# GpSimd multiplies the second halves of eight late units, from copies that ScalarE makes of the y banks

## The chip, the cores and the metric

One core of a Trainium2 chip. The metric is the device time of one execution in microseconds; the median of the runs is compared. TensorE is the matrix engine (PE in the profile), VectorE is DVE, ScalarE is ACT, GpSimd is POOL, SyncE is SP.

## The reference, cut to what matters

A recommendation tower: 40 embedding tables are looked up for 512 samples, every pair of the 40 fields goes through its own 32x32 matrix, and the 780 results with 16 dense features go through three layers. All of it is float32.

```python
e = jnp.stack([tbl_0[ids[:, 0]], ..., tbl_39[ids[:, 39]]], axis=1)   # 512 x 40 x 32
z = jnp.einsum('bpd,pde,bpe->bp', e[:, iidx, :], bilinear_matrices, e[:, jidx, :])   # 780 pairs
h = jnp.concatenate([z, dense_ctx], axis=1)
h = jnp.maximum(h @ W_top1 + b_top1, 0.0)
h = jnp.maximum(h @ W_top2 + b_top2, 0.0)
y = h @ W_top3
```

## The kernel before, in words

The 40 fields are put in 10 groups of four (`GROUPS`, `G`); a group transposed to 128 partitions (4 fields x 32) by 512 samples is one `xt[:, t, :]`. Four groups (`HOT_POS` 0, 1, 3, 5) have small tables and are looked up by one-hot matmuls on TensorE (L515), whose 0/1 columns VectorE makes (L409; four of them ScalarE, L369 and L372). The other six (`GATHER_POS` 2, 4, 6, 7, 8, 9) are gathered by GpSimd: 96 indirect DMAs (L301), 16 to a group, in one row. VectorE then turns such a group with one transpose (L425, the step "turn").

The pairs are done in 50 units (`UNIT`), each a pair of groups (t, u). For unit k TensorE makes y = matrices x xt[u] as four results of 128x512 in float32 (L546): they are two halves, 2k and 2k+1, and a half lies in two PSUM banks. There are three places for halves (`Y_SLOTS`), so half h needs the place of half h-3 (L544). VectorE multiplies each half of 128x1024 by xt[t] into `prod` (L449, 100 instructions), and TensorE sums the products over the 32 rows of each field into z_ps with a selecting matrix (L561, the step "sum"). `prod` has room for four units.

The order is written down as a list (`schedule`): unit k, then sum k-2 (`LAG`), then what `AFTER` puts behind unit k: one-hot rounds, and in the last third the parts of the first layer ("l1", L467 called from L527) on blocks of z that are ready. Behind the sum of the last of eight units ScalarE copies z_ps to z_t (L385, the step "z"); it also takes out the first part of the first layer (L382). VectorE has its own list with the same units in order, the turns (before units 0, 8, 18, 24, 32 and 38) and the "joins" of the first layer (L430). Groups 8 and 9 are t in the last 18 units: unit 32 is (8, 0), unit 33 is (8, 1), up to (8, 7) in unit 39; 40 to 47 are (9, 0) to (9, 7); 48 and 49 are the inner pairs.

Each engine runs its instructions in order. On GpSimd nothing follows the 96 gathers. The tail after unit 49 is the rest of the three layers.

Of the kernel before, what the change touches and what calls it, by code (L numbers as in the profile page):

```python
# [11 lines left out]
ALU = mybir.AluOpType  # L12
# [37 lines left out]
UNIT = []  # L50
# [6 lines left out]
MIX_RING = 2  # L57
# [2 lines left out]
       (2, 0, 3 * DIM, False), (2, 3 * DIM, P, True)]  # L60
HEAD_AFTER = 4


Y_SLOTS = 3
PROD_UNITS = 4
# [28 lines left out]
def first_unit(t):  # L94
# [11 lines left out]
    "l1": [18, 24, 26, 27, 28, 28, 31, 32, 33, 34, 36, 37, 41, 41, 43, 44, 46, 47, 48, 49],  # L106
    "turn": [0, 8, 18, 24, 32, 38],
}


def last_unit(b):
# [55 lines left out]
def bass_dlrm_tower(nc, ids, rows, hot_ids, numbers, negatives, hot_tables, dense, mats, w1, b1, w2, b2, w3, select, out):  # L167
# [23 lines left out]
    vector_rounds = [j for j in range(len(ROUND)) if j not in BY_SCALAR]  # L191
    scalar_rounds = [j for j in range(len(ROUND)) if j in BY_SCALAR]

    def mix_slot(g, s):

        return GROUPS + 3 * (g % (2 * MIX_RING)) + s if s < G - 1 else g ^ 1

    with ExitStack() as ctx:
# [30 lines left out]
        table = sb("table", [P, HOTS, G, MAX_ROWS * DIM])  # L229
        rest = sb("rest", [P, PIECE_RING, G, MAX_ROWS * DIM])  # L230
        low = sb("low", [P, PIECE_RING, G, MAX_ROWS * DIM], BF16)

        layer_cols = hot_id[:].rearrange("p o c -> p (o c)").bitcast(F32)
        h1 = layer_cols[:, 0:M1 * BATCH].rearrange("p (m b) -> p m b", m=M1)
# [42 lines left out]
        t_out = sem("t_out")  # L277
        y_done = sem("y_done")
        prod_done = sem("prod_done")
        sum_done = sem("sum_done")  # L280
        z_out = sem("z_out")
        z_last = sem("z_last")
# [10 lines left out]
        @block.gpsimd  # L293
        def _(pool):
            pool.wait_ge(ids_in, 16)
            nc.gpsimd.tensor_tensor(row[:], ids_sb[:, 0, :], ids_sb[:, 1, :], ALU.add).then_inc(row_done, 1)
            pool.wait_ge(row_done, 1)
            for g in range(GATHERS):
                for c in range(CHUNKS):
                    n = g * CHUNKS + c  # L300
                    pool.indirect_dma_start(out=x_rows[:, g, c, :], out_offset=None, in_=rows,  # L301
                                            in_offset=bass.IndirectOffsetOnAxis(ap=row[:, n:n + 1], axis=0)
                                            ).then_inc(gathered[g], 16)

        @block.sync
        def _(sp):
            def load_mats(c):
                sp.dma_start(m_sb[:, MAT0[c]:MAT0[c + 1], :], mats[:, MAT0[c]:MAT0[c + 1], :]).then_inc(mats_in[c], 16)

            def load_hot_ids(o):  # L310
                sp.dma_start(hot_id[:, o, :], hot_ids[:, o, :]).then_inc(hot_id_in[o], 16)

            def load_tables(o):
                cols = slice(0, HOT_ROWS[o] * DIM)
                sp.dma_start(table[:, o, :, cols], hot_tables[:, o, :, cols]).then_inc(table_in[o], 16)

            sp.dma_start(ids_sb[:], ids).then_inc(ids_in, 16)
            load_hot_ids(0)
            load_tables(0)
            load_hot_ids(1)  # L320
            load_tables(1)
            load_mats(0)
            load_hot_ids(2)
            load_tables(2)
            for c in range(1, 4):
                load_mats(c)
            sp.dma_start(dense_sb[:], dense).then_inc(dense_in, 16)
            for o in range(3, HOTS):
                load_hot_ids(o)
                load_tables(o)  # L330
            for c in range(4, len(MAT_CHUNKS)):
                load_mats(c)
            sp.dma_start(b1_sb[:], b1).then_inc(head_in, 16)
            sp.dma_start(b2_sb[:], b2).then_inc(head_in, 16)
            sp.dma_start(w3_sb[:], w3).then_inc(head_in, 16)

            for g in range(GROUPS):
                if g == HEAD_AFTER:
                    sp.wait_ge(hot_used, len(ROUND))
                    sp.dma_start(w1_sb[:], w1).then_inc(w1_in, 16)  # L340
                    sp.dma_start(w2_sb[:], w2).then_inc(head_in, 16)
                if g >= 2 * MIX_RING:

                    sp.wait_ge(prod_done, 2 * UNIT.index((g - 2 * MIX_RING, g - 2 * MIX_RING)) + 2)
                x_there(sp, g)
                x_there(sp, g ^ 1)
                for part, p0, p1, own in MIX:
                    sp.dma_start(xt[p0:p1, mix_slot(g, part), :],
                                 xt[p0:p1, g if own else g ^ 1, :]).then_inc(mixed[g], 16)
            sp.wait_ge(y_out, 1)  # L350
            sp.dma_start(out.rearrange("(p bt) o -> p (bt o)", bt=BT), y[:]).then_inc(stored, 16)
            sp.wait_ge(stored, 16)

        @block.scalar
        def _(act):
            act.dma_start(number[:], numbers).then_inc(number_in, 16)
            act.dma_start(negative[:], negatives).then_inc(negative_in, 16)
            act.dma_start(sel[:], select).then_inc(sel_in, 16)
            for what, k in steps:
                if what == "hot":  # L360
                    for j in [j for j in scalar_rounds if BY_SCALAR[j] == k]:
                        o, r = ROUND[j]
                        n = scalar_rounds.index(j)
                        act.wait_ge(hot_id_in[o], 16)
                        act.wait_ge(negative_in, 16)
                        if n >= ONES_RING:
                            act.wait_ge(hot_used, scalar_rounds[n - ONES_RING] + 1)
                        columns = ones(j).rearrange("p f b -> p (f b)")
                        nc.scalar.activation(columns, hot_id[:, o, :], ACT.Abs,  # L369
                                             bias=negative[:, n:n + 1]).then_inc(ones_half, 1)  # L370
                        act.wait_ge(ones_half, n + 1)
                        nc.scalar.activation(columns, columns, ACT.Relu, bias=negative[:, len(BY_SCALAR):],  # L372
                                             scale=-1.0).then_inc(ones_done, 1)
                if what == "hot" and ends_bank(what, k):
                    act.wait_ge(hot_used, k + 1)
                    nc.scalar.activation(xt[:, HOT_POS[ROUND[k][0]], :], t_ps[:], ACT.Copy).then_inc(t_out, 1)  # L376
                if what == "l1" and ends_bank(what, k) and L1_STEP[k][0] == 0:
                    m = L1_STEP[k][1]
                    if m == 0:
                        act.wait_ge(head_in, 16 * 4)  # L380
                    act.wait_ge(part_done, m + 1)
                    nc.scalar.activation(h1[:, m, :], t_ps[:], ACT.Identity, bias=b1_sb[:, m:m + 1]).then_inc(t_out, 1)  # L382
                if what == "z" and k < BLOCKS - 1:
                    act.wait_ge(sum_done, last_unit(k) + 1)
                    nc.scalar.activation(z_t[:, k, :], z_ps[:], ACT.Copy).then_inc(z_out, 1)  # L385
            for m in range(M1):
                act.wait_ge(l1_added, m + 1)
                nc.scalar.activation(h1[:, m, :], h1[:, m, :], ACT.Relu).then_inc(l1_out, 1)
            for c in range(M2):
                act.wait_ge(l2_done, c + 1)  # L390
                nc.scalar.activation(h2[:, c, :], y_ps[:, L2_BANK[c], :], ACT.Relu,
                                     bias=b2_sb[:, c:c + 1]).then_inc(l2_out, 1)
            act.wait_ge(l3_done, 1)
            nc.scalar.activation(y[:], t_ps[:, 0:BT], ACT.Copy).then_inc(y_out, 1)  # L394

        @block.vector
        def _(dve):
            nc.vector.memset(prod[:, 0, 0, :], 0.0).then_inc(cleared, 1)  # L398
            dve.wait_ge(number_in, 16)
            for what, k in vector_schedule():  # L400
# [30 lines left out]
                if what == "unit":  # L431
# [9 lines left out]
                    else:  # L441
                        partners = [xt[:, t, :].unsqueeze(1).to_broadcast([P, 2, BATCH])] * 2
                    for half in range(2):
                        slot = (2 * k + half) % Y_SLOTS
                        dve.wait_ge(y_done, 2 * k + half + 1)
                        if half == 0 and k >= PROD_UNITS:

                            dve.wait_ge(sum_done, k - PROD_UNITS + 1)
                        nc.vector.tensor_tensor(prod[:, k % PROD_UNITS, 2 * half:2 * half + 2, :],  # L449
                                                y_ps[:, 2 * slot:2 * slot + 2, :], partners[half],  # L450
                                                ALU.mult).then_inc(prod_done, 1)
# [9 lines left out]
        def _(pe):  # L461
# [9 lines left out]
            def late_blocks(parts):  # L471
                for m in parts:

                    pe.wait_ge(prod_done, LATE_READ[m])
                    for b in range(LATE_BLOCK, BLOCKS - 1):
                        pe.wait_ge(z_out, b + 1)
                        by_columns(y_ps[:, LATE_BANK[m], :], w1_sb[:, b, m * P:(m + 1) * P], z_t[:, b, :],
# [13 lines left out]
            for what, k in steps:  # L491
# [39 lines left out]
                if what == "unit":  # L531
# [6 lines left out]
                    for s in range(G):  # L538
# [2 lines left out]
                        place = INNER_PLACE[s] if t == u else s  # L541
                        if s % 2 == 0 and half >= Y_SLOTS:

                            pe.wait_ge(prod_done, half - Y_SLOTS + 1)  # L544
                        rows = slice(s * DIM, (s + 1) * DIM)
                        last = nc.tensor.matmul(y_ps[:, 2 * slot + place % 2, :], m_sb[rows, k, :], xt[rows, u, :],  # L546
                                                start=True, stop=True)
# [2 lines left out]
                if what == "sum":  # L550
# [3 lines left out]
                        pe.wait_ge(sel_in, 16)  # L554
                    if r == 0 and b >= 1:
                        pe.wait_ge(z_out, b)
                    pe.wait_ge(prod_done, 2 * k + 2)
                    window = sel[:, SEL_COLS - G * r:SEL_COLS - G * r + DIM]
                    for s in range(G):
                        place = INNER_PLACE[s] if UNIT[k][0] == UNIT[k][1] else s  # L560
# [109 lines left out]
```

## Time and profile before

| what | value |
|---|---|
| median of 3 runs | 188.96 us (188.72 to 190.56) |
| span of the profiled execution | 304.4 us |
| busy PE, DVE, ACT, POOL in that span | 210.0, 159.1, 29.8, 95.4 us |
| mean granted TensorE clock in that span | 0.808 |

The profiled execution's time is given by its span alone, and that span is 115.4 us longer than the median of the runs without the profiler. How to read it: a row of the timeline is start, duration, engine, line, operation, output<-inputs, shape, how many were merged, and in brackets how long the engine was idle before it and what ended that. In the chain, which is followed back from the last instruction, a piece that lasts longer than others of its line holds a wait of TensorE.

### The profile page before, as it was taken

How to read it: one execution, taken by the hardware profiler on the slowest of the kernel's cores; microseconds unless marked ns; L12 is line 12 of the kernel's file. 1: busy time of each engine (PE TensorE's matmuls, PEld its weight loads, DVE VectorE, ACT ScalarE, POOL GpSimd, SP SyncE). 2: the span in 40 equal slices, each digit the busy share in tenths (PEclk: the TensorE clock that was granted, in tenths of full speed). 3: DMA queues.
4: the chain of work that ended last, by engine and by line, in shares of the span. 5: the costliest groups of instructions: out<-in, count | busy, mean ns of one | idle time of the engine just before them, and what ended most of it. 6: DMA issues, size and time to landing. Idle time of an engine off the chain costs nothing.

```text
span 304.4 us, 3703 instructions
## 1 busy us (share of the span) xinstructions
PE 210.0 (69%) x1590; PEld 62.3 (20%) x1590; DVE 159.1 (52%) x156; ACT 29.8 (10%) x30; POOL 95.4 (31%) x101
## 2 busy tenths in 40 slices
PE   8866443212221221106999999999999999999997
PEld 3212100000000000002433322322222223222223
DVE  2752000210000000004999999999969889898630
ACT  2905000000000000005000000000110100000032
POOL 4777777777777777500000000000000000000000
PEclk9995755555555555555999999999999999999999
DMA  7992010000100100003550097000510004300000
GB/s 238 395 411 68 13 14 13 13 13 13 15 13 14 14 13 13 11 0 98 163 155 3 8 309 202 2 0 2 156 54 0 2 0 121 89 0 2 2 0 0
DMA packets 12688, 20.19 MB, mean 66 GB/s; under 512 B 3840, under 2 KB 6784, under 8 KB 12544
## 3 DMA queue, kind: packets, MB, share of 16 engines
q1 hardware_dynamic: 9168, 18.33, 18.7%
q0 software_dynamic: 3072, 1.58, 3.2%
q8 instruction: 12, 0.20, 0.3%
q10 hardware_dynamic: 432, 0.05, 0.1%
q14 instruction: 4, 0.03, 0.0%
HBM read 12.08 MB, written 0.00 MB: 40 GB/s over the span
## 4 chain that ended last, share of the span: by engine, by line
PE 69%; issue 30%; DVE 0%; ACT 0%
PE y_ps L546 20%; PE z_ps L561 16%; PE t_ps L515 16%; PE t_ps L467 6%; PE y_ps L467 5%; PE z_ps L483 3%; PE y_ps L490 3%; PE t_ps L583 1%; DVE prod L398 0%; ACT y L394 0%
## 5 line engine op out<-in xcount | busy, mean ns | idle before, releaser
L449 DVE TENSOR_TENSOR prod<-y_ps,xt 128x1024 f32<-128x1024 f32 x100 | 115.8, 1217 | 8.1 <-PE y_ps L546 7.6
L301 POOL DMA_INDIRECT x_rows<-rows,row x96 | 94.8, 988 | 29.2 <-issue 29.0
L409 DVE TENSOR_SCALAR hot<-hot_id,number 128x2048 bf16<-128x2048 int16 x32 | 23.6, 758 | 120.3 <-remote 74.7
L546 PE MATMUL y_ps<-xt,m_sb 32*128 32x512 f32 x400 | 65.0, 640 | 0.0
L561 PE MATMUL z_ps<-prod,sel 128*32 128x512 f32 x400 | 53.2, 604 | 0.0
L515 PE MATMUL t_ps<-hot,table 128*32 128x512 bf16 x128 | 19.5, 441 | 30.3 <-issue 30.0
L546 PEld LDWEIGHTS y_ps<-xt,m_sb 32*128 32x128 f32 x400 | 22.5, 182 | 40.6 <-issue 29.4
L515 PE MATMUL t_ps<-hot,low 128*32 128x512 bf16 x128 | 20.8, 436 | 13.5 <-issue 13.1
L515 PE MATMUL t_ps<-hot,rest 128*32 128x512 bf16 x128 | 19.8, 437 | 11.9 <-issue 11.7
L467 PE MATMUL t_ps<-z_t,table 128*32 128x512 f32 x160 | 20.5, 593 | 0.0
L483 PE MATMUL z_ps<-hot_id,sel 128*32 128x512 bf16 x30 | 9.5, 427 | 15.5 <-issue 15.5
L376 ACT ACTIVATE xt<-t_ps 128x512 f32<-128x512 f32 x4 | 2.4, 597 | 149.5 <-remote 119.8
L561 PEld LDWEIGHTS z_ps<-prod,sel 128*32 128x32 f32 x400 | 8.0, 108 | 37.8 <-issue 24.1
L515 PEld LDWEIGHTS t_ps<-hot,table 128*32 128x32 bf16 x128 | 5.1, 102 | 43.3 <-issue 39.0
L385 ACT ACTIVATE z_t<-z_ps 128x512 f32<-128x512 f32 x6 | 3.6, 597 | 84.2 <-PE z_ps L561 84.2
L515 PE MATMUL t_ps<-z_t,low 128*32 128x512 bf16 x16 | 3.8, 496 | 9.2 <-issue 9.2
L515 PEld LDWEIGHTS t_ps<-hot,low 128*32 128x32 bf16 x128 | 5.4, 105 | 22.0 <-issue 19.8
L515 PEld LDWEIGHTS t_ps<-hot,rest 128*32 128x32 bf16 x128 | 5.1, 103 | 18.5 <-issue 17.1
L490 PE MATMUL y_ps<-prod 128*128 128x512 bf16 x24 | 7.8, 504 | 1.5 <-DVE prod L398 1.5
L515 PE MATMUL t_ps<-z_t,rest 128*32 128x512 bf16 x16 | 3.8, 495 | 7.1 <-issue 7.1
L372 ACT ACTIVATE z_t<-z_t,negative 128x2048 bf16<-128x2048 bf16 x4 | 8.0, 2002 | 0.1
L369 ACT ACTIVATE z_t<-hot_id,negative 128x2048 bf16<-128x2048 int16 x4 | 8.0, 1994 | 0.0
(30 smaller groups left out, 70.5 us busy)
## 6 DMA issues: line engine op xcount, KB each, us to landing
xt<-xt SPq DMA_DIRECT2D x20, 192.0 KB, 2.5
xt<-xt SPq DMA_DIRECT2D x20, 128.0 KB, 2.5
hot_id<-hot_ids SPq DMA_DIRECT2D x4, 512.0 KB, 4.2
table<-w SPq DMA_DIRECT2D x1, 1792.0 KB, 8.2
x_rows<-rows,row POOLq DMA_INDIRECT x96
table<-hot_tables SPq DMA_DIRECT2D x2, 640.0 KB
xt<-xt SPq DMA_DIRECT2D x20, 64.0 KB, 2.1
table<-hot_tables SPq DMA_DIRECT2D x2, 512.0 KB
```

Source lines behind the costliest of these rows:

```text
L301: pool.indirect_dma_start(out=x_rows[:, g, c, :], out_offset=None, in_=rows, in_offset=bass.IndirectOffsetOnAxis(ap=row[:, n:n + 1], axis= ...
L369: nc.scalar.activation(columns, hot_id[:, o, :], ACT.Abs, bias=negative[:, n:n + 1]).then_inc(ones_half, 1)
L372: nc.scalar.activation(columns, columns, ACT.Relu, bias=negative[:, len(BY_SCALAR):], scale=-1.0).then_inc(ones_done, 1)
L385: nc.scalar.activation(z_t[:, k, :], z_ps[:], ACT.Copy).then_inc(z_out, 1)
L409: nc.vector.tensor_scalar(ones(k).rearrange("p f b -> p (f b)"), hot_id[:, o, :], number[:, o, r:r + 1], None, ALU.is_equal).then_inc(hot_ ...
L449: nc.vector.tensor_tensor(prod[:, k % PROD_UNITS, 2 * half:2 * half + 2, :], y_ps[:, 2 * slot:2 * slot + 2, :], partners[half], ALU.mult). ...
L467: last = nc.tensor.matmul(bank[q * DIM:(q + 1) * DIM, :], weights[:, q * DIM:(q + 1) * DIM], columns, start=start, stop=stop, skip_group_c ...
L483: nc.tensor.matmul(z_ps[0:DIM, :], sel[:, 0:SEL_COLS].bitcast(BF16)[:, 0:DIM], hot_id[:, 1, 0:BATCH].bitcast(BF16), start=start, stop=star ...
L490: nc.tensor.matmul(y_ps[:, 0, :], zeros[:, BATCH:BATCH + P], zeros[:, 0:BATCH], start=True, stop=True)
L515: last = nc.tensor.matmul(t_ps[f * DIM:(f + 1) * DIM, :], pieces[piece][:, f, :], ones(k)[:, f, :], start=(r == 0 and piece == 0), stop=(r ...
L546: last = nc.tensor.matmul(y_ps[:, 2 * slot + place % 2, :], m_sb[rows, k, :], xt[rows, u, :], start=True, stop=True)
L561: last = nc.tensor.matmul(z_ps[s * DIM:(s + 1) * DIM, :], window, prod[:, k % PROD_UNITS, place, :], start=first, stop=(k == last_unit(b)) ...
```

## The change

Eight second halves, 2k+1 for k = 33, 35, ..., 47, are no longer multiplied by VectorE. ScalarE copies the two banks of such a half to SBUF (`y_copy`, which lies in the space of `rest`, with room for two copies), and GpSimd multiplies the copy by xt[t] in two instructions of 128x512 each. TensorE takes the place of such a half again when it is copied, and sums such a unit when both VectorE's and GpSimd's part are done. GpSimd's multiplications stand behind its 96 gathers. ScalarE's copy of unit k stands ahead of the z copy and the first-layer step that follow unit k.

The pieces are, in order: the constants, two helpers, the space of the copies, GpSimd behind its gathers, ScalarE, VectorE, and TensorE's wait in a unit and in a sum.

```diff
+POOL_HALF = {2 * k + 1 for k in range(33, 48, 2)}
+COPY_RING = 2
...
+    def half_read(engine, h):
+        if h in POOL_HALF:
+            engine.wait_ge(y_copied, halves_before(h + 1, True))
+        else:
+            engine.wait_ge(prod_done, halves_before(h + 1, False))
+
+    def unit_multiplied(engine, k):
+        engine.wait_ge(prod_done, halves_before(2 * k + 2, False))
+        if halves_before(2 * k + 2, True):
+            engine.wait_ge(pool_prod_done, halves_before(2 * k + 2, True))
...
+        y_copy = rest[:].rearrange("p o f c -> p (o f c)")[:, 0:COPY_RING * 2 * BATCH].rearrange(
+            "p (n h b) -> p n h b", n=COPY_RING, h=2)
...
+            for n, h in enumerate(sorted(POOL_HALF)):
+                k = h // 2
+                t, u = UNIT[k]
+                x_there(pool, t)
+                pool.wait_ge(y_copied, n + 1)
+                pool.wait_ge(sum_done, k - PROD_UNITS + 1)
+                for place in range(2):
+                    last = nc.gpsimd.tensor_tensor(prod[:, k % PROD_UNITS, 2 + place, :], y_copy[:, n % COPY_RING, place, :],
+                                                   xt[:, t, :], ALU.mult)
+                last.then_inc(pool_prod_done, 1)
...
             for what, k in steps:
+                if what == "unit" and 2 * k + 1 in POOL_HALF:
+                    n = halves_before(2 * k + 1, True)
+                    slot = (2 * k + 1) % Y_SLOTS
+                    act.wait_ge(y_done, 2 * k + 2)
+                    if n >= COPY_RING:
+                        act.wait_ge(pool_prod_done, n - COPY_RING + 1)
+                    elif n == 0:
+                        act.wait_ge(hot_used, len(ROUND))
+                    nc.scalar.activation(y_copy[:, n % COPY_RING, :, :], y_ps[:, 2 * slot:2 * slot + 2, :],
+                                         ACT.Copy).then_inc(y_copied, 1)
...
                     for half in range(2):
+                        if 2 * k + half in POOL_HALF:
+                            continue
...
-                            pe.wait_ge(prod_done, half - Y_SLOTS + 1)
+                            half_read(pe, half - Y_SLOTS)
...
-                    pe.wait_ge(prod_done, 2 * k + 2)
+                    unit_multiplied(pe, k)
```

GpSimd's queue in the kernel before, from its first instruction on data to its end:

```order
L296 TENSOR_TENSOR row<-ids_sb 128x96 [waits ids_in]
L301 DMA x_rows<-rows,row 128x32 [waits row_done]
L301 DMA x_rows<-rows,row 128x32 x95
L198 UNCONDITIONAL_BRANCH
```

And in the changed kernel, the same place and the first two of the eight pairs (`rest` is the space in which the copies lie):

```order
L322 TENSOR_TENSOR row<-ids_sb 128x96 [waits ids_in]
L327 DMA x_rows<-rows,row 128x32 [waits row_done]
L327 DMA x_rows<-rows,row 128x32 x95
L337 TENSOR_TENSOR prod<-rest,xt 128x512 [waits sum_done,y_copied,turned]
L337 TENSOR_TENSOR prod<-rest,xt 128x512
L337 TENSOR_TENSOR prod<-rest,xt 128x512 [waits sum_done,y_copied,turned]
L337 TENSOR_TENSOR prod<-rest,xt 128x512
```

The pairs stand behind all 96 gathers, not behind those alone that they need.

TensorE in the kernel before, from unit 35 to sum 34 (L546 is a unit's matmul, L561 a sum's, the last row is the first-layer step behind unit 36):

```order
L546 MATMUL y_ps<-xt,m_sb 128x512 [waits prod_done]
L546 MATMUL y_ps<-xt,m_sb 128x512
L546 MATMUL y_ps<-xt,m_sb 128x512 [waits prod_done]
L546 MATMUL y_ps<-xt,m_sb 128x512
L561 MATMUL z_ps<-prod,sel 32x512 [waits prod_done]
L561 MATMUL z_ps<-prod,sel 32x512 x3
L546 MATMUL y_ps<-xt,m_sb 128x512 [waits prod_done]
L546 MATMUL y_ps<-xt,m_sb 128x512
L546 MATMUL y_ps<-xt,m_sb 128x512 [waits prod_done]
L546 MATMUL y_ps<-xt,m_sb 128x512
L561 MATMUL z_ps<-prod,sel 32x512 [waits prod_done]
L561 MATMUL z_ps<-prod,sel 32x512 x3
```

The same rows in the changed kernel (L594 is the unit's matmul, L609 the sum's):

```order
L594 MATMUL y_ps<-xt,m_sb 128x512 [waits y_copied]
L594 MATMUL y_ps<-xt,m_sb 128x512
L594 MATMUL y_ps<-xt,m_sb 128x512 [waits prod_done]
L594 MATMUL y_ps<-xt,m_sb 128x512
L609 MATMUL z_ps<-prod,sel 32x512 [waits pool_prod_done,prod_done]
L609 MATMUL z_ps<-prod,sel 32x512 x3
L594 MATMUL y_ps<-xt,m_sb 128x512 [waits prod_done]
L594 MATMUL y_ps<-xt,m_sb 128x512
L594 MATMUL y_ps<-xt,m_sb 128x512 [waits prod_done]
L594 MATMUL y_ps<-xt,m_sb 128x512
L609 MATMUL z_ps<-prod,sel 32x512 [waits pool_prod_done,prod_done]
L609 MATMUL z_ps<-prod,sel 32x512 x3
```

Nothing on TensorE moves. The first half of unit 35 waits for ScalarE's copy, and the sum behind unit 35, sum 33, is the first that waits for GpSimd.

ScalarE in the kernel before, from the first-layer step behind unit 28 to its copy of z behind sum 47:

```order
L382 ACTIVATE hot_id<-t_ps,b1_sb 128x512 [waits part_done]
L385 ACTIVATE z_t<-z_ps 128x512 [waits sum_done]
L382 ACTIVATE hot_id<-t_ps,b1_sb 128x512 [waits part_done] x2
L385 ACTIVATE z_t<-z_ps 128x512 [waits sum_done] x2
```

And in the changed kernel:

```order
L428 ACTIVATE hot_id<-t_ps,b1_sb 128x512 [waits part_done]
L404 ACTIVATE rest<-y_ps 128x1024 [waits hot_used,y_done]
L431 ACTIVATE z_t<-z_ps 128x512 [waits sum_done]
L428 ACTIVATE hot_id<-t_ps,b1_sb 128x512 [waits part_done]
L404 ACTIVATE rest<-y_ps 128x1024 [waits y_done]
L404 ACTIVATE rest<-y_ps 128x1024 [waits pool_prod_done,y_done]
L428 ACTIVATE hot_id<-t_ps,b1_sb 128x512 [waits part_done]
L404 ACTIVATE rest<-y_ps 128x1024 [waits pool_prod_done,y_done] x2
L431 ACTIVATE z_t<-z_ps 128x512 [waits sum_done]
L404 ACTIVATE rest<-y_ps 128x1024 [waits pool_prod_done,y_done] x3
L431 ACTIVATE z_t<-z_ps 128x512 [waits sum_done]
```

Eight copies come in; from the third on they wait for GpSimd, and what follows them on ScalarE waits with them.

## Rows read from the trace of the kernel before

**Rows 1.** The page: span, busy time, busy tenths and clock in 40 slices.

```profile
span 304.4 us, 3703 instructions
PE 210.0 (69%) x1590; PEld 62.3 (20%) x1590; DVE 159.1 (52%) x156; ACT 29.8 (10%) x30; POOL 95.4 (31%) x101
...
POOL 4777777777777777500000000000000000000000
PEclk9995755555555555555999999999999999999999
```

**Rows 2.** Stretches: us, busy PE, PEld, DVE, ACT, POOL, clock, DMA share, GB/s.

```profile
3.50:25.00 21.50, 15.29 (x123) 5.13 (x121) 12.46 (x15) 9.57 (x6) 16.88 (x16) 0.97 1.00 374
...
5.47:150.44 144.97, 54.11 (x357) 15.67 (x355) 28.13 (x33) 18.76 (x12) 93.22 (x95) 0.60 0.24 72
28.30:139.24 110.94, 27.29 (x79) 5.27 (x71) 6.80 (x8) 0.84 (x2) 75.27 (x79) 0.52 0.08 12
```

**Rows 3.** The chain from unit 33 to unit 46: start, us, what.

```profile
237.42 1.07 PE y_ps L546 x8
...
244.34 0.99 PE z_ps L561 x8
245.34 1.45 PE y_ps L546 x8
...
247.78 0.86 PE t_ps L467 x8
...
253.63 1.45 PE y_ps L546 x8
...
256.07 1.27 PE y_ps L546 x8
...
258.33 1.30 PE y_ps L546 x8
259.64 1.00 PE z_ps L561 x8
...
264.48 1.45 PE y_ps L546 x8
...
272.77 1.45 PE y_ps L546 x8
```

**Rows 4.** Timeline of POOL, the gathers 1, 11 and 96.

```profile
3.55 1.09 POOL L301 DMA_INDIRECT x_rows<-rows,row  x1 [0.28 <-POOL row L296]
...
17.78 1.53 POOL L301 DMA_INDIRECT x_rows<-rows,row  x1 [0.30 <-issue]
...
125.99 1.37 POOL L301 DMA_INDIRECT x_rows<-rows,row  x1 [0.30 <-issue]
```

**Rows 5.** Timeline of DVE: a table split, twenty products in a row, the last turn.

```profile
17.27 1.22 DVE L418 TENSOR_TENSOR rest<-table 128x1024 f32<-128x1024 f32 x1
...
175.57 22.90 DVE L449 TENSOR_TENSOR prod<-y_ps,xt 128x1024 f32<-128x1024 f32 x20
...
252.01 0.70 DVE L425 STREAM_TRANSPOSE xt<-x_rows 128x512 f32<-128x512 f32 x1
```

**Rows 6.** Groups: line, engine, shapes, count, busy, mean ns, idle before.

```profile
L449 DVE TENSOR_TENSOR prod<-y_ps,xt 128x1024 f32<-128x1024 f32 x100 | 115.8, 1217 | 8.1 <-PE y_ps L546 7.6
...
L409 DVE TENSOR_SCALAR hot<-hot_id,number 128x2048 bf16<-128x2048 int16 x32 | 23.6, 758 | 120.3 <-remote 74.7 <-issue 32.8 <-PE t_ps L515 8.5
...
L369 ACT ACTIVATE z_t<-hot_id,negative 128x2048 bf16<-128x2048 int16 x4 | 8.0, 1994 | 0.0
...
L376 ACT ACTIVATE xt<-t_ps 128x512 f32<-128x512 f32 x4 | 2.4, 597 | 149.5 <-remote 119.8 <-PE t_ps L515 29.7
L454 DVE TENSOR_TENSOR z_t<-z_ps,dense_sb 128x512 f32<-128x512 f32 x1 | 0.7, 691 | 2.3 <-PE z_ps L561 2.3
...
L296 POOL TENSOR_TENSOR row<-ids_sb 128x96 int32<-128x96 int32 x1 | 0.4, 382 | 2.4 <-DMA ids_sb<-ids 2.4
```

**Rows 7.** Timeline of ACT: the copy of z behind sum 39.

```profile
260.70 0.60 ACT L385 ACTIVATE z_t<-z_ps 128x512 f32<-128x512 f32 x1 [8.38 <-PE z_ps L561]
```

More of the change, by code:

```diff
@@ L108, with halves_before @@
 }
+def halves_before(n, by_pool):
+    return len([h for h in range(n) if (h in POOL_HALF) == by_pool])
 def last_unit(b):
@@ L279, in bass_dlrm_tower @@
         prod_done = sem("prod_done")
+        y_copied = sem("y_copied")
+        pool_prod_done = sem("pool_prod_done")
         sum_done = sem("sum_done")
@@ L342, in _ @@
                 if g >= 2 * MIX_RING:
-                    sp.wait_ge(prod_done, 2 * UNIT.index((g - 2 * MIX_RING, g - 2 * MIX_RING)) + 2)
+                    unit_multiplied(sp, UNIT.index((g - 2 * MIX_RING, g - 2 * MIX_RING)))
                 x_there(sp, g)
@@ L472, in late_blocks @@
                 for m in parts:
-                    pe.wait_ge(prod_done, LATE_READ[m])
+                    half_read(pe, LATE_READ[m] - 1)
                     for b in range(LATE_BLOCK, BLOCKS - 1):
```

## The prediction

> **What bounds the kernel now.** I read the page first. It shows a span of 304.4 us, in which GpSimd works through the first 17 of 40 slices and TensorE runs at half its clock in most of that time [rows 1]. The runs without the profiler take 188.96 us. So the profiled execution holds some 115 us that the timed runs don't, and the next view must say where. The busy time by stretches does: from 28.3 to 139.2 us TensorE has 79 matmuls, VectorE 8 operations and ScalarE 2, while GpSimd gathers on at its even pace [rows 2]. The reader is to see that the one-hot stage is stretched in the profile and GpSimd's gathers are not. Everything about who is early or late at the units therefore has to be moved to the timed run's clock before it is used.
>
> The shift has two bounds. It is at least 304.4 - 188.96 = 115.4 us. And from VectorE's first operation on data (5.47) to the first product (150.44) VectorE is busy 28.1 of 145.0 us [rows 2]; that work can't be shorter than itself, so at most 145.0 - 28.1 = 116.8 us go. I take 116.1. That the bounds lie so close also says that the timed run has next to no other waits.
>
> The third view is the chain that ended last. From unit 33 on it is TensorE's in every piece: 1.07 us for a unit, 1.00 for a sum, 0.86 for a first-layer step. Six units last longer: 1.45, 1.45, 1.27, 1.30, 1.45 and 1.45 [rows 3], together 8.37 - 6 x 1.07 = 1.95 us. They stand where no first-layer step comes between, and VectorE, at 22.90/20 = 1.145 us a half [rows 5], needs 2.29 us for a unit against TensorE's 2.07. Elsewhere a unit with a step takes TensorE 2.93 us, and VectorE waits for it. So the late stage is bound by TensorE, and VectorE's share in it is 1.95 us.
>
> **The change, part by part.**
>
> Removed: eight multiplications of 1.217 us on VectorE [rows 6]. Only what TensorE waited for can be won. Two units without a step cost TensorE 2 x 2.07 = 4.14 us and VectorE now 3 x 1.145 = 3.4, so all six waits should go: -1.95 us. This is the most that the change can bring, 1.0%. It loses all of it if the waits had another cause.
>
> Added on ScalarE: eight copies of 128x1024 out of PSUM. The trace has 597 ns for 512 columns and 1994 for 2048 [rows 6]; on the line between them 1024 columns take 1.06 us, and the bounds are 0.60 and 1.99. That is no longer than VectorE's 1.217, and ScalarE takes the half at once, where VectorE has a backlog, so the place comes free no later. Behind the copy of unit 41 stands the copy of z that follows sum 39. The half is there when the unit's piece ends, at 258.33 + 1.30 = 259.63; the copy would end at 260.75, and z would start at 260.8 where it starts at 260.70 [rows 7]. The next reader of that z is the second of two first-layer steps, 0.86 us behind 260.64 [rows 3]. z is then there at about 261.4, the step begins at 261.5: hidden, with 0.1 us to spare. The other z copies follow theirs by several microseconds.
>
> Added on GpSimd: sixteen multiplications of 128x512 in float32. None is in the trace. The nearest row is its own two-input add of 96 columns in 382 ns [rows 6]. Taken in full proportion that is 2.04 us for 512 columns, the upper bound; VectorE's 691 ns for 512 columns [rows 6] is the lower. VectorE's two sizes, 691 for 512 and 1217 for 1024, leave 0.17 us that is fixed; with as much fixed on GpSimd, (382 - 165)/96 = 2.26 ns a column gives 0.17 + 1.16 = 1.3 us. I take that, 2.6 us for a pair. Between y and the sum a pair then costs 1.06 + 2.6 us and about 0.3 for three hand-overs (z starts 0.06 behind its sum, rows 3 and 7; I take 0.1 each): 3.96 us. In place of it TensorE has, behind unit 39, where it is tightest, sum, unit, sum and unit of 1.00 + 1.07 + 1.00 + 1.07 = 4.14 us; elsewhere one first-layer step more (5.0) or two (5.9). Hidden, once GpSimd is on time.
>
> Moved: nothing, but the pairs are queued behind all 96 gathers, and this is the term that decides. In the quiet stretch a gather is 75.27/79 = 0.95 us [rows 2] and 0.30 before the next [rows 4]; the last ends at 125.99 + 1.37 = 127.4. In the timed run GpSimd starts its gathers at the same time and has no reason to be earlier. TensorE however comes to sum 33, the first that needs a GpSimd pair, at 244.34 - 116.1 = 128.2 [rows 3]. The copy of unit 33 is long there (unit 33 ends at 238.49 - 116.1 = 122.4). So GpSimd begins its first pair when its last gather is issued and TensorE waits for both multiplications.
>
> When is that in the timed run? While VectorE is busy with tables and one-hot columns the gathers are slower: 16 in 21.5 us, 1.34 each against 1.25 [rows 2], one of 1.53 beside the split of a table [rows 4, 5]. That is 1.4 us for 12.5 us of VectorE's work. In the timed run some 22 us more of such work fall into the time of the gathers (28.1 us ahead of the first product less these 12.5, and nine one-hot rounds of 0.758 us among the units [rows 2, 6]): 0 to 2.4 us, as it is VectorE or the full DMA queues of the start that slows them. I take half, 1.2: free at 128.6.
>
> The Trainium skill, page "SBUF — State Buffer", section "Who interferes with whom", says that VectorE in a mode that uses both its ports shuts GpSimd out for the whole instruction, and that a VectorE instruction with at most one SBUF input outside these modes doesn't contend. The row agrees in its direction, 1.53 us for a gather against 0.95 in the quiet stretch [rows 2, 4]. By the rule the full 2.4 us would be due for the one-hot work, and nothing for the products, which read one input from PSUM: 1.2 us more than I take, 191.4. No row shows a gather beside a product.
>
> Wait at sum 33: 128.6 + 2.6 + 0.2 - 128.2 = 3.2 us. Behind it TensorE gives GpSimd 5.0 us to each of the next sums with a pair, and the second pair starts where the first ends, so the delay is paid once.
>
> Sum for a timed run: +3.2 - 1.95 = +1.2 us (rounded). Against the profiled execution's own 304.4 us only the gain counts, since there GpSimd is free before the units begin. Its span should fall by up to 2 us, apart from the stretch, which may differ from one profile to the next. Against the median it is 188.96 + 1.2 = 190.2 us.
>
> **The rivals.**
>
> *GpSimd is on time.* Without the profiler the gathers may be quicker than 1.25 us; the stretched stage proves that the profile disturbs this kernel. With GpSimd free by 125.4 nothing waits at sum 33, and the time is 188.96 - 1.95 = 187.0. For it: only that doubt. Against: in the quiet stretch nothing holds GpSimd up (VectorE nearly idle, DMA share 0.08 [rows 2]), so 1.25 us a gather looks like its own work. The last turn, at 252.01 - 116.1 = 135.9 [rows 5], bounds the gathers only from above: it forbids them to end later than about 134.
>
> *GpSimd multiplies slowly, and later sums wait too.* At 2.04 us a multiplication, a pair with copy and hand-overs needs 5.4 us. Sum 33 then waits 128.6 + 4.1 + 0.2 - 128.2 = 4.7; sums 37 and 45 (5.0 us of cover) 0.4 each, sum 39 (4.14) 1.3. Together 6.8 - 1.95 = +4.9, 193.9. It decides from a multiplication of (4.14 - 1.36)/2 = 1.39 us on; below that only sum 33 is left. For it: the proportion to the only GpSimd arithmetic in the trace. Against: small operations carry a fixed part.
>
> *The gain doesn't come.* If the six long units waited for something other than VectorE's products, only the wait at sum 33 is left: 192.2. Against: a long unit with its sum lasts 2.27 to 2.45 us, where VectorE's two products take 2.29.
>
> **How the numbers follow.** The forecast, late by one wait, has 0.55; its own range is 188.2 (gathers at 127.4, shift 115.4: a wait of 1.2) to 193.5 (gathers 2.4 later, 2.04 a multiplication, shift 116.8: a wait of 6.7 less 1.95, rounded down since not all come together). On time 0.20, slow multiplication 0.15, no gain 0.05, and 0.05 for something between on time and late. A measurement of this kernel tells about 1% from no change, 187.07 to 190.85. Faster: a half of "on time" and little else, 0.12. Slower: all of the slow multiplication, the missing gain, and a third of the forecast, 0.40. Within: 0.48. The range 186.9 to 193.5 leaves out the lower part of "on time" and the upper half of the slow multiplication.
>
> **What would show it.** In the changed profile: the six long units at 1.07; copies of about 1.06 us on ScalarE; pairs on GpSimd of 2.6 us that start right behind a copy, and hence no wait at sum 33 in the profiled execution, its part from the first unit to the end shorter by 1.9 us. If the timed median falls by as much, the gathers end earlier than I say; if it rises while the profile's units get shorter, the wait at sum 33 exists in the timed run only. Wrong would be the whole sum if GpSimd's pair lasts over 2.8 us in the profile and sum 39 waits there.

## The result, and the profile after

| kernel | median | runs | ratio to before, 95% interval |
|---|---|---|---|
| before | 188.84 us | 188.70 to 190.56 (4) | |
| changed | 193.26 us | 192.88 to 194.16 (4) | 1.023, 1.019 to 1.026 |

The change costs 4.4 us. This time the profiled execution has the length of the others: its span is 191.5 us and its time 193.29, so 1.8 us lie around the span, and the one-hot stage isn't stretched. The timeline can be read as it stands. The page of the changed kernel, rows as in [rows 1] and the groups that the change touches:

```profile
span 191.5 us, 3749 instructions
...
PE 183.1 (96%) x1590; PEld 57.5 (30%) x1590; DVE 149.1 (78%) x148; ACT 37.9 (20%) x38; POOL 115.9 (61%) x117
...
PEclk9999999999999999999999999996999999999999
...
L497 DVE TENSOR_TENSOR prod<-y_ps,xt 128x1024 f32<-128x1024 f32 x92 | 107.0, 1218 | 19.0 <-PE y_ps L594 17.7
L327 POOL DMA_INDIRECT x_rows<-rows,row x96 | 95.1, 990 | 29.2 <-issue 28.6
...
L609 PE MATMUL z_ps<-prod,sel 128*32 128x512 f32 x400 | 53.9, 611 | 2.9 <-POOL prod L337 2.9
...
L337 POOL TENSOR_TENSOR prod<-rest,xt 128x512 f32<-128x512 f32 x16 | 20.3, 1288 | 20.3 <-issue 14.7
...
L404 ACT ACTIVATE rest<-y_ps 128x1024 f32<-128x1024 f32 x8 | 8.2, 1026 | 43.1 <-PE y_ps L594 43.1
```

The reader is to see three things. A GpSimd multiplication took 1.29 us and a copy on ScalarE 1.03, close to the 1.3 and 1.06 of the sum. TensorE waited once for GpSimd, 2.9 us, in a sum. And the row of the clock has a 6 in one slice where all others are 9. The chain around that slice (start, us, what) shows both:

```profile
123.23 0.50 PE y_ps L594
123.73 0.30 issue
...
126.53 0.94 POOL x_rows L327
...
127.50 2.50 POOL prod L337 x2
130.01 0.14 issue
130.14 1.28 PE z_ps L609 x8
131.42 2.02 PE y_ps L594 x8
133.44 1.42 PE z_ps L609 x8
134.86 0.86 PE t_ps L515 x8
```

The chain leaves TensorE, runs through GpSimd's last gathers and its first two multiplications, and comes back to TensorE at sum 33 (130.14), where unit 35 had ended at 127.22. Behind it a sum, a unit and a sum take 1.28, 2.02 and 1.42 us instead of 1.00, 1.07 and 1.00. The busy time by stretches (columns as in [rows 2]) gives the reason, TensorE's granted clock:

```profile
127.15:130.14 2.99, 0.07 (x4) 0.03 (x1) 1.23 (x1) 1.02 (x1) 2.96 (x4) 1.00 0.03 6
130.14:134.86 4.72, 4.72 (x28) 1.15 (x32) 1.39 (x2) 0.00 (x0) 2.35 (x2) 0.64 0.00 0
134.86:170.00 35.14, 35.14 (x272) 9.21 (x264) 24.75 (x23) 7.43 (x8) 15.27 (x12) 1.00 0.16 46
```

The first stretch still holds the last 0.07 us of unit 35, so TensorE is without work for 2.92 us. Then come 4.72 us at a clock of 0.64 on average: taken in smaller pieces it is 1.00 up to 130.6, 0.50 (that is 1.2 GHz) from 131.0 to 134.0, and 1.00 (2.4 GHz) again from 134.4. The fall comes behind the wait, when TensorE is at work again. The price is 4.72 less the 1.00 + 1.07 + 1.00 of a sum, a unit and a sum elsewhere, 1.65 us. And the long units that answer to [rows 3] are all there but the one that lies in that stretch:

```profile
140.71 1.45 PE y_ps L594 x8
...
143.15 1.27 PE y_ps L594 x8
...
145.41 1.31 PE y_ps L594 x8
...
151.56 1.45 PE y_ps L594 x8
...
159.86 1.45 PE y_ps L594 x8
```

So: +2.92 for the wait, +1.65 for the clock, -0.38 for the wait of unit 36, which goes under in it, together +4.2 of the measured 4.4 us. VectorE has eight products less and TensorE won nothing by it.

### The profile page after: what moved, and what is told of

The parts are those of the page before. It is cut to its first block, busy times and chain, and to the rows that moved or that the text cites. A ratio compares the mean times of both kernels' runs of the same rounds, so it can differ in the third digit from the quotient of the medians.

```text
span 191.5 us, 3749 instructions
## 1 busy us (share of the span) xinstructions
PE 183.1 (96%) x1590; PEld 57.5 (30%) x1590; DVE 149.1 (78%) x148; ACT 37.9 (20%) x38; POOL 115.9 (61%) x117
## 4 chain that ended last, share of the span: by engine, by line
PE 77%; DVE 14%; POOL 3%; DMA 3%; issue 2%; SPq 0%; ACT 0%; DVEq 0%
PE y_ps L594 30%; PE z_ps L609 26%; PE t_ps L515 9%; DVE hot L455 8%; PE y_ps L515 7%; PE t_ps L563 3%; DMA table<-hot_tables 3%; DVE rest L464 3%; DVE low L466 2%; POOL x_rows L327 1%; POOL prod L337 1%; DVE prod L497 1%; PE t_ps L631 1%; PE z_ps L531 0%; SPq L347 0%
## 5 line engine op out<-in xcount | busy, mean ns | idle before, releaser
L497 DVE TENSOR_TENSOR prod<-y_ps,xt 128x1024 f32<-128x1024 f32 x92 | 107.0, 1218 | 19.0 <-PE y_ps L594 17.7
L594 PE MATMUL y_ps<-xt,m_sb 32*128 32x512 f32 x400 | 65.7, 649 | 0.0
L609 PE MATMUL z_ps<-prod,sel 128*32 128x512 f32 x400 | 53.9, 611 | 2.9 <-POOL prod L337 2.9
L594 PEld LDWEIGHTS y_ps<-xt,m_sb 32*128 32x128 f32 x400 | 22.5, 185 | 40.7 <-issue 33.8
L337 POOL TENSOR_TENSOR prod<-rest,xt 128x512 f32<-128x512 f32 x16 | 20.3, 1288 | 20.3 <-issue 14.7
L455 DVE TENSOR_SCALAR hot<-hot_id,number 128x2048 bf16<-128x2048 int16 x32 | 22.4, 754 | 4.1 <-DMA hot_id<-hot_ids 4.1
L609 PEld LDWEIGHTS z_ps<-prod,sel 128*32 128x32 f32 x400 | 8.0, 108 | 41.5 <-issue 33.1
L404 ACT ACTIVATE rest<-y_ps 128x1024 f32<-128x1024 f32 x8 | 8.2, 1026 | 43.1 <-PE y_ps L594 43.1
L563 PE MATMUL t_ps<-hot,table 128*32 128x512 bf16 x128 | 13.4, 384 | 1.6 <-DVE low L466 1.2
L563 PE MATMUL t_ps<-hot,rest 128*32 128x512 bf16 x128 | 13.3, 379 | 0.0
L563 PE MATMUL t_ps<-hot,low 128*32 128x512 bf16 x128 | 13.3, 379 | 0.0
L515 PEld LDWEIGHTS t_ps<-z_t,table 128*32 128x32 f32 x160 | 5.1, 111 | 12.5 <-issue 11.7
L515 PE MATMUL y_ps<-z_t,table 128*32 128x512 f32 x64 | 7.2, 592 | 0.0
L531 PE MATMUL z_ps<-hot_id,sel 128*32 128x512 bf16 x30 | 7.1, 379 | 0.0
L515 PE MATMUL y_ps<-hot_id,w_sb 128*32 128x512 f32 x64 | 7.0, 592 | 0.0
```

Of the source, the lines that this page charges most:

```text
L337: last = nc.gpsimd.tensor_tensor(prod[:, k % PROD_UNITS, 2 + place, :], y_copy[:, n % COPY_RING, place, :], xt[:, t, :], ALU.mult)
L404: nc.scalar.activation(y_copy[:, n % COPY_RING, :, :], y_ps[:, 2 * slot:2 * slot + 2, :], ACT.Copy).then_inc(y_copied, 1)
L455: nc.vector.tensor_scalar(ones(k).rearrange("p f b -> p (f b)"), hot_id[:, o, :], number[:, o, r:r + 1], None, ALU.is_equal).then_inc(hot_ ...
L515: last = nc.tensor.matmul(bank[q * DIM:(q + 1) * DIM, :], weights[:, q * DIM:(q + 1) * DIM], columns, start=start, stop=stop, skip_group_c ...
L531: nc.tensor.matmul(z_ps[0:DIM, :], sel[:, 0:SEL_COLS].bitcast(BF16)[:, 0:DIM], hot_id[:, 1, 0:BATCH].bitcast(BF16), start=start, stop=star ...
L563: last = nc.tensor.matmul(t_ps[f * DIM:(f + 1) * DIM, :], pieces[piece][:, f, :], ones(k)[:, f, :], start=(r == 0 and piece == 0), stop=(r ...
```

## The experiments

The question was why the long units stay. The new theory, here "latency": with three places for halves, the second half of unit k (2k+1) takes the place of half 2k-2, the first half of the unit before. Only a sum of 1.00 us lies between those units where no first-layer step does, and the product of that first half ends 1.22 us and a hand-over behind its unit. Second halves are not what TensorE waits for. The rival is the prediction's own, "throughput": VectorE as a whole is too slow. The kernel before ran again beside each group of experiments, with medians of 189.07 us (beside the first four) and 188.90 (beside the last three); each ratio is to those runs.

**Six halves, units 37 to 47**, without those of units 33 and 35, whose copies are made before the gathers end.

```diff
-POOL_HALF = {2 * k + 1 for k in range(33, 48, 2)}
+POOL_HALF = {2 * k + 1 for k in range(37, 48, 2)}
```

> Six halves (units 37 to 47) instead of eight: the first pair is needed at sum 37, some 10 us behind the last gather. Latency theory (the second half of a unit takes the place of the FIRST half of the unit before, whose product VectorE still makes 1.2 us after it is there, so the six long units of TensorE stay): no wait for GpSimd, no gain either, 188.8 us, ratio 1.000, units 39, 40, 41, 43, 46 still 1.45, 1.27, 1.30, 1.45, 1.45. Throughput theory of the prediction (VectorE's 2.29 us a unit against 2.07): these five waits of 1.58 us go, 187.3 us, ratio 0.992.

Measured: 188.96 us, ratio 1.000 (0.998 to 1.003). From the chain of this kernel:

```profile
136.34 1.45 PE y_ps L594 x8
...
138.78 1.26 PE y_ps L594 x8
...
141.05 1.31 PE y_ps L594 x8
...
147.20 1.45 PE y_ps L594 x8
...
155.49 1.45 PE y_ps L594 x8
```

No wait for GpSimd, no gain. The throughput theory's 187.3 us doesn't come: six products less leave the five waits to 0.01 us as they were.

**Only the half of unit 33.**

```diff
-POOL_HALF = {2 * k + 1 for k in range(33, 48, 2)}
+POOL_HALF = {2 * 33 + 1}
```

> Only the half of unit 33 goes to GpSimd, behind all its gathers. If the whole loss hangs on the one wait at sum 33: 3.0 us of wait, 1.6 us of slower matmuls behind it (granted clock below 1 for a moment), less 0.4 of a wait that is hidden, so 193.2 us, ratio 1.023, as with all eight. If the other seven pairs had a share of the loss: below 192.

Measured: 192.32 us, ratio 1.017 (1.011 to 1.024), and four runs that lie 2.5 us apart: 193.25 and 192.89 at a mean granted clock of 0.991, 191.74 and 190.73 at 1.000 and 0.999. The profiled one is that of 191.74, and its stretch around the wait is:

```profile
127.15:130.18 3.03, 0.07 (x5) 0.04 (x2) 2.35 (x2) 0.00 (x0) 2.86 (x3) 1.00 0.04 6
130.18:134.25 4.07, 4.07 (x36) 1.04 (x40) 1.90 (x2) 0.00 (x0) 0.00 (x0) 1.00 0.00 0
```

Of the 3.03 us the first 0.07 are unit 35's, so the wait is 2.96, about the 2.92 of all eight halves, and the clock stays at 1.00. So the wait at sum 33 is made by this one half, and the clock follows it in some executions and not in others. Where it fell, the time is that of all eight halves; the seven other pairs cost nothing. Why the run of 190.73 is 1.0 us shorter than the profiled one at the same clock is open: it has no profile. The expectation was right on the place and too firm on the clock.

The mean clock of the runs without a profile says how often it falls without this wait: of 78 runs of kernels that don't have it (before beside the experiments, the six halves above and the last four kernels below), 76 are at 0.995 or more; one of before, 190.78 us, is at 0.990 and one of the run with six halves, 190.97 us, at 0.991. So such a fall can come without the wait, but it is rare there, and with the wait it came in 4 of 4 and in 2 of 4 runs.

**TensorE kept busy in the wait.** Three matmuls with weights of zero are added into z_ps ahead of sum 33.

```diff
+                    if k == 33:
+                        for _ in range(3):
+                            nc.tensor.matmul(z_ps[0:SEL_COLS, :], sel[:, 0:SEL_COLS], xt[:, 8, :],
+                                             start=False, stop=False, skip_group_check=True)
                     unit_multiplied(pe, k)
```

> The changed kernel with three float32 matmuls of 128x28 weights that are all zero, added into z_ps ahead of sum 33 (some 2.5 us of TensorE work in place of idling; the result is the same). If the slow matmuls behind the wait come from TensorE having been idle: the clock stays at 1.00, 1.6 us come back, 191.6 us, ratio 1.015. If they come from something else (GpSimd reading beside them, say): still 193.3, ratio 1.023, or more by what the three matmuls last beyond the wait.

Measured: 191.54 us, ratio 1.013 (1.011 to 1.015), all four runs within 0.3 us and none below a clock of 0.996. TensorE's timeline (columns as in [rows 4]):

```profile
127.05 2.76 PE L607 MATMUL z_ps<-xt,sel 128*28 128x512 f32 x6
130.10 1.06 PE L613 MATMUL z_ps<-prod,sel 128*32 128x512 f32 x8 [0.29 <-POOL prod L337]
131.10 1.14 PE L594 MATMUL y_ps<-xt,m_sb 32*128 32x512 f32 x8
```

Sum 33 starts at the same 130.1, and what follows runs at full pace although GpSimd multiplies its second pair beside it. With the idling gone no run of four falls, where all four of the changed kernel did, and 1.7 us come back: the idling was what took the clock down.

**The first pair ahead of the last four gathers** (`pair` is the body of GpSimd's loop over the halves).

```diff
+                    if (g, c) == (GATHERS - 1, EARLY_PAIR):   # EARLY_PAIR = 11
+                        pair(0, sorted(POOL_HALF)[0])
```

> All eight pairs, but the pair of unit 33 is issued by GpSimd ahead of its last four gathers, when the copy has just been made (about 122.5 us). If the wait at sum 33 is the gathers' place in the queue: no wait there, the pair of unit 35 is ready at about 132.7 and waited for by 0.3 us at most; 188.8 to 189.3 us, ratio 1.000 to 1.002. If GpSimd's multiplications are late for another reason: 192 or more. If the throughput theory holds: 187.3.

Measured: 189.27 us, ratio 1.000 (0.998 to 1.002). GpSimd's timeline:

```profile
121.94 0.94 POOL L339 DMA_INDIRECT x_rows<-rows,row  x1 [0.30 <-issue]
123.01 2.54 POOL L329 TENSOR_TENSOR prod<-rest,xt 128x512 f32<-128x512 f32 x2
125.69 0.98 POOL L339 DMA_INDIRECT x_rows<-rows,row  x1
...
130.43 2.54 POOL L329 TENSOR_TENSOR prod<-rest,xt 128x512 f32<-128x512 f32 x2
```

All eight pairs are on GpSimd and the whole loss is gone: it was the place in the queue, behind gathers that nobody needed yet (the last group is turned before unit 38). Sum 35 now waits 0.15 us for the second pair (unit 37 ends at 132.96, the sum starts at 133.11), less than the 0.3 that were allowed for. The gain is missing as before.

**First halves, and second halves of the same units**, to set the two theories against each other with the same amount of work.

```diff
-POOL_HALF = {2 * k + 1 for k in range(33, 48, 2)}
+POOL_HALF = {2 * k for k in (38, 39, 40, 42, 45)}        # the first run
+POOL_HALF = {2 * k + 1 for k in (38, 39, 40, 42, 45)}    # the second
```

> ScalarE copies and GpSimd multiplies the FIRST halves of units 38, 39, 40, 42 and 45 (those that are followed by a unit without a first-layer step between; GpSimd is past its gathers there). Latency theory: the place that the next unit's second half needs is free after a copy of 1.03 us instead of a product of 1.22, so each of the waits behind these units gets 0.19 us shorter (1.45 to 1.26, the 1.27 and 1.30 to 1.1): -0.9 us, ratio 0.995. Throughput theory: VectorE has as many products less as in the next run, so both give the same time.

> The same five units, but their second halves. Latency theory: no change, ratio 1.000, long units at 1.45, 1.27, 1.30, 1.45, 1.45. Throughput theory: the same as the run with the first halves, and below before.

Measured: first halves 188.07 us, ratio 0.995 (0.994 to 0.997); second halves 188.83 us, ratio 1.000 (0.999 to 1.001). The chain of the run with first halves, units 39, 40, 41, 43 and 46:

```profile
136.92 1.24 PE y_ps L594 x8
...
139.16 1.07 PE y_ps L594 x8
...
141.23 1.24 PE y_ps L594 x8
...
147.32 1.25 PE y_ps L594 x8
...
155.41 1.24 PE y_ps L594 x8
```

1.45 became 1.24, by the 0.2 us that a copy (1.03) is shorter than a product (1.22). The two in the middle didn't both fall to 1.1, as was expected: unit 40 lost its whole wait and unit 41 kept 0.17 of its 0.24. In the run with second halves units 39, 43 and 46 stayed at 1.45, unit 40 fell to 1.07 and unit 41 rose to 1.50: there throughput had a share (the run with six halves left the product of unit 38's second half on VectorE, and unit 40 stayed at 1.26), but what unit 40 won unit 41 lost again. The intervals of the two runs don't touch.

**The first half split between two engines.** ScalarE copies bank 0 for GpSimd, VectorE multiplies bank 1, in the six units ahead of a long one.

```diff
-POOL_HALF = {2 * k + 1 for k in range(33, 48, 2)}
+POOL_HALF = {2 * k for k in (35, 38, 39, 40, 42, 45)}
...
+                        if 2 * k + half in POOL_HALF:
+                            nc.vector.tensor_tensor(prod[:, k % PROD_UNITS, 1, :], y_ps[:, 2 * slot + 1, :],
+                                                    xt[:, t, :], ALU.mult).then_inc(prod_done, 1)
+                            continue
```

> The first half of units 35, 38, 39, 40, 42 and 45 is taken out of PSUM by two engines at once: ScalarE copies its first bank (0.60 us), which GpSimd multiplies in one instruction of 1.27 us, and VectorE multiplies its second bank (0.69 us). Latency theory: the place is free 0.7 to 0.8 us behind the unit, before the sum of 1.00 us is through, so all six waits go: -1.95 us, 186.9 us, ratio 0.990. Throughput theory: VectorE has 6 x 0.53 = 3.2 us less to do, less than the five or eight halves of 1.22 us taken from it in the other runs, so no more gain than theirs. If the first GpSimd product (unit 35, y there at 127 us) is late: a wait of at most 0.3 us.

Measured: 187.16 us, ratio 0.991 (0.990 to 0.993). The chain from unit 38 to unit 41, and what three engines do behind unit 38:

```profile
134.04 1.07 PE y_ps L594 x8
...
136.11 1.07 PE y_ps L594 x8
...
138.17 1.07 PE y_ps L594 x8
...
140.24 1.07 PE y_ps L594 x8
```

```profile
135.15 0.60 ACT L402 ACTIVATE rest<-y_ps 128x512 f32<-128x512 f32 x1 [0.35 <-PE y_ps L594]
135.15 0.69 DVE L494 TENSOR_TENSOR prod<-y_ps,xt 128x512 f32<-128x512 f32 x1
...
135.87 1.28 POOL L335 TENSOR_TENSOR prod<-rest,xt 128x512 f32<-128x512 f32 x1 [6.62 <-ACT rest L402]
```

The place is free at 135.84, the next unit begins at 136.11, and every unit is at 1.07. With six instructions on GpSimd instead of sixteen this version is faster than before and than the changed kernel.

## Why the prediction was right in its sign and wrong in its sum

190.2 us was forecast and 193.26 measured; the range of 186.9 to 193.5 held it, near its end. That it did is luck: its upper end was made of later gathers and slower multiplications, and neither came; the missing gain and the clock, which did, took their room. The wait of 6.7 us at that end is also added up wrongly, 6.5 by its own terms (129.8 + 4.1 + 0.2 less 127.5), which with -1.95 is the 193.5 without any rounding down.

*The wait at sum 33* was the step that decided, and it was right: 3.2 us forecast, 2.92 measured. That the size fits is luck too, for two of its parts were wrong by over 1 us and took each other away. The last gather ended at 127.47, where I took 128.6 after 127.4 plus 1.2 for VectorE's one-hot work. And the shift was 117.2 (304.4 less 187.2, the median less the 1.8 around the span), where I took 116.1 and held 116.8 for the most. The pair took 2.50 (2.6).

The bound on the shift failed because VectorE's busy time in that stage can be shorter than I held: from the first one-hot round to the first product the changed kernel's profile has 27.84 us, of which VectorE is busy 26.72, where the stretched one has 28.13. One comparison (L409, L455) is nearly the same in both, 764 and 747 ns on the mean of 23; but back to back their records overlap, six in 4.18 us at 24.68, so that all 23 are busy for 15.8 us and not for 17.2.

The 1.2 us for slower gathers were wrong in another way. The gathers of the changed kernel are slower beside the comparisons, and not beside products. Three of GpSimd's rows, and VectorE's beside them (a third gather beside the comparisons, at 51.48, took 1.03):

```profile
39.93 0.94 POOL L327 DMA_INDIRECT x_rows<-rows,row  x1 [0.30 <-issue]
...
48.67 1.14 POOL L327 DMA_INDIRECT x_rows<-rows,row  x1 [0.30 <-issue]
50.12 1.05 POOL L327 DMA_INDIRECT x_rows<-rows,row  x1 [0.30 <-issue]
```

```profile
36.89 6.96 DVE L497 TENSOR_TENSOR prod<-y_ps,xt 128x1024 f32<-128x1024 f32 x6
...
48.95 3.44 DVE L455 TENSOR_SCALAR hot<-hot_id,number 128x2048 bf16<-128x2048 int16 x5
```

It isn't the DMA queues: their share is 0.11 from 48.6 to 52.4 and 0.31 from 36.9 to 48.6. By stretches, the first two of the changed kernel, the last of before, in which VectorE was nearly idle:

```profile
25.00:54.00 29.00, 28.49 (x316) 10.44 (x308) 28.68 (x32) 2.12 (x2) 22.36 (x22) 1.00 0.43 118
54.00:110.00 56.00, 56.00 (x417) 16.25 (x420) 53.95 (x49) 3.26 (x6) 42.51 (x45) 1.00 0.42 113
```

```profile
25.00:54.00 29.00, 15.10 (x77) 4.08 (x78) 2.02 (x3) 4.10 (x3) 22.16 (x23) 0.56 0.09 13
```

GpSimd's busy time in the 29 us is the same, but it makes 22 gathers in it and not 23. The 21 that start there took 1.04 us on the mean, against 0.95 for those of before, 1.7 us in all. At the end of the queue nothing is left of it, because the profile before held as much elsewhere: its first 16 gathers took 0.5 us longer than the changed kernel's, and those from 54 us on 0.963 us on the mean against 0.942, 1.2 us in all; the last one, 1.37 us [rows 4], stood beside a comparison at 125.78. So my 127.4 already held as much slowing as the gathers of the timed run turn out to have, and the 1.2 came on top of it.

By the rule of the Trainium skill, page "SBUF — State Buffer", section "Who interferes with whom", a VectorE instruction that uses both its ports shuts GpSimd out for its whole length. The rows agree in the direction, 1.03 to 1.14 us for the gathers beside five comparisons in a row, but a gather loses 0.1 to 0.2 us there, not the 0.7 of a comparison, and no row tells whether the comparison is such an instruction. The gather of 1.53 us that I took for the rule's row stood beside the split of a table. The rule's other half, no contention with one SBUF input, agrees as well: 42.51 us for the 45 gathers from 54 to 110, nearly all beside products, 0.94 us each.

*"Removed", -1.95 us, is the step that failed.* "So all six waits should go" was drawn from a comparison of rates, 2.29 us for VectorE against 2.07 for TensorE. The rates didn't even fit four of the six: a unit of 1.45 with its sum lasts 2.45 us, not 2.29. A latency of 1.22 us plus a hand-over less 1.00 of cover gives their 0.38. The line of the kernel that frees a place (half h waits for half h-3) would have told which half is waited for. The runs with six halves and with five second halves gave nothing of it (ratio 1.000 in both), and the six waits went only when the first halves were split. The rival "the gain doesn't come" had it right and got 0.05.

*The clock* was in no term: +1.65 us in the profiled execution, and all four runs of the changed kernel have a mean clock of 0.982 to 0.991.

*The later pairs* cost nothing, as forecast: from the third on a pair starts every 4.5 us or more against 2.5 needed, and the long units from 39 on are to 0.01 us as before.

*That the profiled execution would show no wait* was wrong for a plain reason: the stretch of the profile before didn't come back. Of nine profiled executions in this study only that one had it.

## What to carry to other kernels

Before work is taken from a busy engine, ask for each wait of the bounding engine which instruction ends it, by the line that waits, and not whether the rates agree; only that instruction is worth shortening, and moving its neighbours gives nothing. Work for an idle engine takes its place in that engine's queue: look up what stands ahead of it there and when that ends, on the clock of the timed runs. And a wait that is put on a TensorE that never waited may be paid twice, once as the wait and once as a slower clock behind it. Last, before a busy time is compared between two stretches, count the instructions in each: the same busy time can hold fewer of them.

## What the runs showed of the hardware that was not expected

A wait of 2.92 us on TensorE after some 120 us of nearly unbroken work was followed by a fall of the clock in one profile: 4.7 us at a mean granted clock of 0.64, with 3 us of it at 0.50. In another profile with a wait of 2.96 us it didn't fall at all; the four runs of that second kernel split into two at 0.991 and two at 0.999 or more, some 1.8 us apart on the mean. With 2.76 us of the wait filled by matmuls the clock stayed at 0.996 or more in all four runs. What decides in which executions it falls stays open.

GpSimd's indirect gathers took 0.94 us each beside products that VectorE reads from PSUM, and 1.03 to 1.14 us beside five one-hot comparisons in a row, int16 in and bf16 out, that VectorE makes from one SBUF tile into another.

What stretched the one-hot stage of the profile before to 111 us, with GpSimd's gathers at their normal 1.25 us beside it, stays open.
